# Side work of a fused attention and FP4 block set at other places in its slots, and two of three zeroings of K tiles put later in the start

## What is computed

```
xn   = layernorm(x)                                  # no gain, no bias, eps 1e-5
q    = rope(xn @ Wqa @ Wqb)   16 heads of 8          # low-rank projections
k, v = xn @ Wkva @ Wkvb       4 heads of 8; k = rope(k)
attn = softmax(causal(q k' / sqrt(8))) v @ Wout + bout
fp4(t): blocks of 16 along the last dim, scale = max|t| / 6,
        round |t| / scale to 0, .5, 1, 1.5, 2, 3, 4, 6, times sign and scale
ffn  = fp4(silu(fp4(xn) fp4(Wgate)') * (fp4(xn) fp4(Wup)')) fp4(Wdown)'     # 352 hidden
out  = x + attn + ffn
```

## Time and profile before

| | us |
|---|---|
| median of 3 runs (788.24 to 791.44) | 790.27 |
| the profiled execution, whole | 788.24 |
| its span, first to last instruction | 785.8 |

### The profile page before, as it was taken

How to read it: one execution, slowest core, us unless ns; L and a number is a source line. 1 busy time by engine, 2 the same in 40 slices (tenths; PEclk the granted TensorE clock), 3 DMA queues, 4 the chain that set the end, 5 groups by cost and what they waited for, 6 DMA issues and landing times.

```text
span 785.8 us, 18291 instructions
## 1 busy us (share of the span) xinstructions
PE 718.4 (91%) x6453; PEld 440.8 (56%) x6453; DVE 627.7 (80%) x1424; ACT 535.9 (68%) x1154; POOL 588.6 (75%) x630
## 2 busy tenths in 40 slices
PE   2467899999999999999999999999999999999886
PEld 1233455665656565665656565665656565665443
DVE  6569888889798888989798888989798888878412
ACT  2213676867777777867777777877777777777772
POOL 4533597878879797868889797878788797856662
PEclk9999899999999999999999999999999999999999
DMA  4432224334334433344334334243334333241111
GB/s 111 108 77 82 67 76 109 93 106 113 99 93 117 103 114 97 94 106 113 97 94 119 104 109 105 89 117 104 96 99 126 94 117 95 77 115 46 57 50 49
DMA packets 84885, 75.41 MB, mean 96 GB/s; under 512 B 28627, under 2 KB 66868, under 8 KB 84796
## 3 DMA queue, kind: packets, MB, share of 16 engines
q1 hardware_dynamic: 84796, 74.25, 35.1%
HBM read 40.38 MB, written 27.25 MB: 86 GB/s over the span
## 4 chain that ended last, share of the span: by engine, by line
PE 62%; DVE 15%; ACT 7%; POOL 6%; issue 4%; DMA 3%; SPq 2%; POOLq 0%; DVEq 0%; ACTq 0%
PE pv_ps L1159 16%; PE exp_ps L1137 12%; PE max_ps L1122 8%; DVE neg_max L732 7%; PE misc_ps L1183 5%; PE max_ps L1123 5%; PE misc_ps L1220 5%; ACT P L958 3%; PE misc_ps L1191 3%; PE misc_ps L1208 3%; PE misc_ps L1218 2%; POOL P L555 2%; PE misc_ps L1169 1%; DVE h_mag L694 1%; PE misc_ps L1187 1%
## 5 line engine op out<-in xcount | busy, mean ns | idle before, releaser
L732 DVE TENSOR_REDUCE neg_max<-max_ps 128x1 f32<-128x512 f32 (+3 forms) x768 | 430.4, 593 | 88.2 <-PE max_ps L1123 86.1
L958 ACT ACTIVATE P<-exp_ps 128x512 f32<-128x512 f32 x512 | 294.7, 599 | 164.0 <-PE exp_ps L1137 163.0
L1137 PE MATMUL exp_ps<-Q,K 128*128 128x512 bf16 (+3 forms) x1024 | 243.4, 301 | 10.2 <-ACT P L958 6.8
L1122 PE MATMUL max_ps<-K,Q 128*128 128x384 bf16 (+2 forms) x768 | 198.9, 278 | 20.1 <-DMA Kd<-K 10.5
L1123 PE MATMUL max_ps<-Kd,Q 128*128 128x128 bf16 x1024 | 190.7, 220 | 1.4 <-DVE neg_max L732 1.2
L555 POOL TENSOR_SCALAR_AFFINE_SELECT P<-P 128x512 f32<-128x512 f32 x256 | 161.7, 667 | 30.6 <-ACT P L961 30.6
L1159 PE MATMUL pv_ps<-P,V 128*32 128x512 f32 (+3 forms) x2048 | 163.9, 438 | 1.2 <-POOL P L555 0.8
L1122 PEld LDWEIGHTS max_ps<-K,Q 128*128 128x128 bf16 x768 | 75.6, 99 | 97.6 <-DVE neg_max L732 53.8
L1123 PEld LDWEIGHTS max_ps<-Kd,Q 128*128 128x128 bf16 x1024 | 99.0, 100 | 42.5 <-issue 22.7
L1137 PEld LDWEIGHTS exp_ps<-Q,K 128*128 128x128 bf16 x1024 | 79.6, 98 | 48.0 <-ACT P L958 26.4
L586 POOL TENSOR_TENSOR h<-gate_sb,up_half 128x352 f32<-128x352 f32 x64 | 59.5, 930 | 54.6 <-DVE gate_sb L745 54.5
(11 more groups left out here) (126 smaller groups left out, 962.7 us busy)
## 6 DMA issues: line engine op xcount, KB each, us to landing
Q<-q_scr SPq DMA_DIRECT2D x64, 224.0 KB
o_scr<-oT SPq DMA_DIRECT2D x31, 256.0 KB, 3.3
q_scr<-q_split SPq DMA_DIRECT2D x16, 384.0 KB, 2.6
Kd<-K SPq DMA_DIRECT2D x64, 96.0 KB
x_in<-x SPq DMA_DIRECT2D x16, 256.0 KB, 4.7
q_scr<-q_split SPq DMA_DIRECT2D x16, 256.0 KB, 2.9
x_res<-x SPq DMA_DIRECT2D x16, 256.0 KB, 5.7
out<-y SPq DMA_DIRECT2D x32, 128.0 KB, 4.4
```

The costliest lines, as they stand in the source:

```text
L732: nc.vector.tensor_reduce(neg_max[:, pr // 4, heads[0]:heads[0] + len(heads), pr % 4, i], max_ps[r % 3][:, 0:len(heads) * n].rearrange("p ...
L958: nc.scalar.activation(P[g % 2][:, hh + r % 2, col:col + 512], ps[:, :], ACT.Exp, scale=SCALE).then_inc(exp_done, 1)
L1122: nc.tensor.matmul(ps[:, col:col + d], Qt, Kt[:, half, g, 0:d], start=True, stop=True)
L1137: last = nc.tensor.matmul(exp_ps[n % 2][:, col:col + width], K[par][:, half, pr // 2, kb * 128:(kb + 1) * 128], Q[par][:, pr, kb * 128:S], ...
```

## The change

Seven edits, none of which changes what is computed:

- DVE, start: of the three zeroings only K[1]'s stays ahead of the iterations. K[0] is cleared in iteration -3 behind var_eps, Kd in the same iteration behind the scales of x.
- DVE, statistics: two of the four bn_stats move to the end of slot 1, with the wait for x; bn_aggr and var_eps move ahead of one more reduction each; a new `neg_mean` (-1 times the mean) is made beside var_eps.
- POOL: `shift` = neg_mean times rstd is computed there, behind the power, instead of on DVE in front of slot 5.
- DVE, slot 0: the x magnitudes go behind the sixth reduction instead of the fifth. ACT: the cast x_mag goes from behind exp tile 0 to behind exp tile 2.
- DVE, slot 4: one reduction is put between the two halves of the h magnitudes.
- ACT: the four h_mag casts each move one place later.
- PE, slot 3: the first three v chunks each move one tile later.

```diff
-H_POWERS = [(2, 2), (2, 3), (2, 4), (3, 2)]
+H_POWERS = [(2, 3), (2, 4), (3, 2), (3, 4)]
...
-                T.wait(pool, var_done, 1, 3, 1)
+                T.wait(pool, var_done, 2, 3, 2)
                 nc.gpsimd.tensor_tensor(rstd[:, :], var_eps[:, :], half_neg[:, :], ALU.pow).then_inc(rstd_done, 1)
+                T.wait(pool, rstd_done, 2, 3, 1)
+                nc.gpsimd.tensor_tensor(shift[:, :], neg_mean[:, :], rstd[:, :], ALU.mult).then_inc(rstd_done, 1)
...
+            def clear_keys(k):
+
+                nc.vector.memset(k[:, :, :, :].bitcast(F32), 0.0).then_inc(k_zeroed, 1)
...
                 reduces(0, 4)
+                reduces(0, 5)
                 if T.has(2):
                     T.wait(dve, x_powers, 1, 2, 1)
                     magnitudes(lambda s, n: T.wait(dve, s, 2, 2, n), x_mag[:, :], x_mags)
-                reduces(0, 5)
...
                 reduces(1, 5)
+                if T.has(3):
+                    T.wait(dve, x_loaded, 16, 3, 16)
+                    for c in range(2):
+                        nc.vector.bn_stats(bn_raw[:, c, :], x_in[:, c, :]).then_inc(bn_done, 1)
...
                 if T.has(3):
-                    T.wait(dve, x_loaded, 16, 3, 16)
-                    for c in range(NT):
+                    for c in range(2, NT):
                         nc.vector.bn_stats(bn_raw[:, c, :], x_in[:, c, :]).then_inc(bn_done, 1)
                 reduces(3, 2)
                 gated(T, 2)
-                reduces(3, 3)
                 if T.has(3):
                     for c in range(NT):
                         T.wait(dve, bn_done, NT, 3, c + 1)
                         dve.sem_inc(dve_marks, 1)
                         nc.vector.bn_aggr(bn_mv[:, c, :], bn_raw[:, c, :]).then_inc(mv_done, 1)
-                reduces(3, 4)
+                reduces(3, 3)
                 if T.has(3):
                     T.wait(dve, mv_done, NT, 3, NT)
 
                     T.wait(dve, rstd_done, 2, 2, 1)
+                    T.wait(dve, rstd_done, 2, 2, 2)
+                    nc.vector.tensor_scalar(neg_mean[:, :], bn_mv[:, :, 0], -1.0, None, ALU.mult).then_inc(var_done, 1)
                     nc.vector.tensor_scalar(var_eps[:, :], bn_mv[:, :, 1], EPS, None, ALU.add).then_inc(var_done, 1)
+                if T.t0 == FIRST_T:
+
+                    clear_keys(K[0])
+                reduces(3, 4)
                 reduces(3, 5)
...
-                    magnitudes(lambda s, n: T.wait(dve, s, 2, 0, n), h_mag[:, :], h_mags)
-                reduces(4, 1, 2)
+                    magnitude_bits(h_mag[:, :], h_mags)
+                reduces(4, 1)
+                if T.has(0):
+                    magnitude_floor(lambda s, n: T.wait(dve, s, 2, 0, n), h_mag[:, :], h_mags)
+                reduces(4, 2)
...
-                if T.has(3):
-                    T.wait(dve, rstd_done, 2, 3, 1)
-                    nc.vector.scalar_tensor_tensor(shift[:, :], bn_mv[:, :, 0], -1.0, rstd[:, :],
-                                                   ALU.mult, ALU.mult).then_inc(rstd_done, 1)
...
                     scales(lambda s, n: T.wait(dve, s, 4, 3, n), x_max[:, :], x_scale[:, :], x_inv[:, :], x_scales)
+                if T.t0 == FIRST_T:
+                    clear_keys(Kd)
...
-            for k in (K[0], K[1], Kd):
-                nc.vector.memset(k[:, :, :, :].bitcast(F32), 0.0).then_inc(k_zeroed, 1)
+            clear_keys(K[1])
...
-                if (slot, r) == (0, 0) and T.has(2):
+                if (slot, r) == (0, 2) and T.has(2):
                     T.wait(act, x_scaled, 1, 2, 1)
...
                     values = slot == 3 and T.has(2)
+                    max_tile(T, slot, 4)
                     if values:
                         value_chunk(T, 0)
-                    max_tile(T, slot, 4)
+                    exp_tile(T, slot, 4)
                     if values:
                         value_chunk(T, 1)
-                    exp_tile(T, slot, 4)
+                    max_tile(T, slot, 5)
                     if values:
                         value_chunk(T, 2)
-                    max_tile(T, slot, 5)
```

More of the change, by code:

```diff
@@ L173, in build @@
         rstd = sb("rstd", [128, NT])
+        neg_mean = sb("neg_mean", [128, NT])
         shift = sb("shift", [128, NT])
@@ L685, in scales, with magnitude_bits, magnitude_floor, magnitudes @@
                 nc.vector.tensor_scalar(inv, inv, 1.0 - 2.0 ** -22, None, ALU.mult).then_inc(sem_, 1)
-            def magnitudes(eng_wait, mag, sem_):
+            def magnitude_bits(mag, sem_):
                 m = mag.bitcast(U16)
                 nc.vector.tensor_scalar(m, m, 0x7F80, 0x0040, ALU.bitwise_and, ALU.bitwise_or).then_inc(sem_, 1)
+            def magnitude_floor(eng_wait, mag, sem_):
                 eng_wait(sem_, 1)
                 nc.vector.tensor_scalar(mag, mag, 1.5 * 2.0 ** 22, None, ALU.max).then_inc(sem_, 1)
+            def magnitudes(eng_wait, mag, sem_):
+                magnitude_bits(mag, sem_)
+                magnitude_floor(eng_wait, mag, sem_)
             def weight_scales():
```

## The result

| | before | after |
|---|---|---|
| median, us (5 runs each) | 789.1 (788.24 to 791.44) | 794.5 (793.42 to 795.95) |
| ratio of after to before, with its 95% interval | | 1.0063 (1.0048 to 1.0078) |
| the profiled execution, whole | 788.24 | 793.81 |
| its span | 785.8 | 791.6 |

The changed kernel is 0.63% slower. The stretches of its trace, in the same order as in the earlier trace rows (start, iteration -1, fourteen batches, t0 = 3, t0 = 5), are these; columns are length, then busy us of PE, weight loads, DVE, ACT and POOL, then clock, DMA share and GB/s. Some of PE's records are missing from this trace (396 of 403 in a batch), so its busy time isn't compared.

The account below looks back on a forecast made before the run. The start was taken as one chain, slots 3 to 7 as bound by GpSimd's chain. Terms 8.3 - 0.35 + 0.3 + 0 - 0.3 - 0.1 = +7.9 us gave 796.1 profiled, 798 median; range 791 to 804.

Parts of the forecast that it names:

- the last batches: The last batches of the kernel: a gain of 0.1 us in the sum.
- the middle outcome: Time within about 4 us of no change, 786.3 to 794.2: Rival (i) and Rival (iv), chance 0.18.
- (a): Start: moving two zeroings ends the scales at 13.5, not 14.47, but SyncE's constants issue 1.95 us later.
- (b): Start, t0 = -2: early statistics wait for batch 1's x, moving q_sin from 22.21 to 30.5, +8.3 us.
- Rival (iv): Start: batch 1's x arrives in time, so the statistics' stall doesn't come; 789.5 us, chance 0.03.
- (c): Batch t0 = -1: x_mag bits behind the sixth reduction, after GpSimd's product is over; 0.35 us gained.
- (d): Slot 0 of every batch: later x_mag cast lets up_half come earlier; 0.29 us gained a batch.
- (e): Slots 3 to 7: GpSimd's longer chain costs 0.3 us a batch; TensorE's savings become waiting ahead of hqT0.
- Rival (iii): Slot 3: var_eps falls into q_split in most batches, 0.67 us more each; 806 us, chance 0.12.
- (f): Other batches: t0 = 0 +0.3 us; t0 = 1 to 12 0; t0 = 5's stall perhaps not recurring, -0.3.
- Rival (i): Steady batches gain after all, -6 us in 12 batches, about outweighing the start; 792 us, chance 0.16.

Follow-up runs that it names:

- Experiment 2: The changed kernel with all three zeroings ahead of the iterations again, the early statistics kept in slot 1; 791.87 us, ratio 1.0042.
- experiment 1: The changed kernel with all four bn_stats back in slot 3 in iteration t0 = -2 alone; 785.82 us, ratio 0.9965.
- Experiment 4: The kernel before with only the x magnitudes moved (cast behind exp tile 2, bits behind the sixth reduction); 787.19 us, ratio 0.9977.
- experiment 7: The kernel before with only the negated mean added on VectorE and the shift product moved to GpSimd; 793.02 us, ratio 1.0036.
- experiments 9: Changed kernel with t0 = -2 statistics back in slot 3, GpSimd's last masks split around h's product, slot 3's value chunks one tile earlier; 778.78 us, ratio 0.9858.
- 10: Changed kernel with t0 = -2 statistics back in slot 3, GpSimd's last masks split, h magnitudes' floor behind slot 4's third reduction; 777.28 us, ratio 0.9839.
- Experiments 3: The changed kernel with the shift product issued twice on GpSimd, the second behind the first; 798.8 us, ratio 1.0126.
- Experiment 8: The changed kernel with t0 = -2 statistics back in slot 3 and the four h_mag casts at their old places; 786.89 us, ratio 0.9959.

## Why the prediction was right, and where it was off

Slower was right, by the mechanism forecast, and the time is in the range. The sum had +7.9 us for the profiled execution (796.1); it took 793.81, +5.6. My 798 had 2 us more on top, for a median that lay above the profiled run by 2.0; with five runs of each kernel that distance was 0.9 before and 0.7 after. So of the 3.5 us that I was over, 2.3 are the sum's and 1.2 come from the step to the median, for which three executions were a thin base. The sum came nearer than its terms did: the start, t0 = -1, t0 = 0, t0 = 5 and the other eleven batches were each taken too high, by 2.8 us in all, and the last batches too low by 0.7. That these errors work against each other is luck. (The chance of the middle outcome is given as 0.18; its parts, 0.16 and 0.03, make 0.19.)

**(a) Zeroings.** Right. The copy at 7.04 (6.95 forecast), the scales' end at 13.55 (13.5), SyncE's constants at 15.71 (15.7). The point I left open, whether the K[0] clear would hold GpSimd, is decided: the power began at 9.03, the zeroing at 9.31, and the power took 1.02 us. Experiment 2 prices the slip at 2.2 us of the stall, where the slip alone (13.73 to 15.71) is 2.0.

**(b) The statistics' wait.** Right in place, kind and nearly in size: q_sin at 30.04 for 30.5, +7.8 us for +8.3. The step that was too long: I took 11.78 us from the first constant's issue to x's, as in the earlier trace rows, and it was 11.08 (11.16 in experiment 2). The issuing takes 8.4 us in all three; the landing of the constants, for which SyncE waits, ended 3.4 us behind it before and 2.7 us in both others. The wait for x's landing gave 0.24 us of this back (2.84 for 2.6). The idle stretch of "some 10 us" was 10.35, the first reduction moved by 7.73, the first max tile to 51.99 (52.5 forecast), and experiment 1 took 8.45 us off with this one edit. Rival (iv) is gone: x is still issued behind the constants.

**(c) t0 = -1.** -0.56 for -0.35. The bits of x_mag took 0.31 us in the new place, as forecast (0.29 beside an idle GpSimd, against 0.64 in the earlier trace rows). But the bits don't explain the stretch. Experiment 4 has them short (0.29) and t0 = -1 longer than before (37.93); experiment 7 has them at 0.64 as before and t0 = -1 at 36.78, 0.57 shorter. So what shortened it is open, and that the term came out near is no proof of it.

**(d) Slot 0.** Right: -0.33 for -0.29. The transposes of xn now follow their exp pair in 0.21 us, where the earlier trace rows had 0.51:

```profile
222.63 0.38 PE L1158 MATMUL exp_ps<-Q,K 128*128 128x384 bf16 x2
222.84 0.61 PE L1208 MATMUL misc_ps<-ident,xn 128*128 128x128 f32 x4
```

Experiment 4 shows it alone (-0.33 in slot 0, -0.34 in the period).

**(e) Slots 3 to 7.** The sum was right (+0.24 for +0.3: 27.68 to 27.92), and so was its reason: GpSimd from q_split's start to h's end takes 18.72 us, and 18.48 in the earlier trace rows (234.62 to 253.10). Its parts fell differently. From the batch t0 = 3, to be laid beside the earlier trace rows:

```profile
239.62 0.39 PE L1158 MATMUL exp_ps<-Q,K 128*128 128x256 bf16 x2 [0.28 <-ACT P L979]
239.77 0.93 POOL L587 TENSOR_TENSOR h<-gate_sb,up_half 128x352 f32<-128x352 f32 x1 [0.18 <-DVE gate_sb L758]
240.34 0.39 DVE L895 TENSOR_SCALAR neg_mean<-bn_mv 128x4 f32<-128x4 f32 x1
240.64 0.16 DVE L896 TENSOR_SCALAR var_eps<-bn_mv 128x4 f32<-128x4 f32 x1
241.03 1.16 POOL L647 TENSOR_TENSOR q_split<-q_rest,q_split 128x512 bf16<-128x512 f32 x1 [0.33 <-ACT q_split L1074]
242.15 2.68 POOL L556 TENSOR_SCALAR_AFFINE_SELECT P<-P 128x512 f32<-128x512 f32 x4
242.88 0.87 DVE L693 TENSOR_SCALAR h_mag<-h_mag 128x1408 uint16<-128x1408 uint16 x1
244.27 0.94 DVE L698 TENSOR_SCALAR h_mag<-h_mag 128x1408 bf16<-128x1408 bf16 x1
245.72 0.29 PE L1144 MATMUL max_ps<-Kd,Q 128*128 128x128 bf16 x2 [0.20 <-DVE neg_max L745]
246.55 0.20 POOL L608 TENSOR_TENSOR shift<-neg_mean,rstd 128x4 f32<-128x4 f32 x1
257.16 2.59 POOL L572 TENSOR_TENSOR h<-h,h_scale 128x1408 f32<-128x1408 f32 x1
259.89 0.52 PE L1229 MATMUL misc_ps<-ident,h 128*128 128x128 f32 x3
```

Slot 3 is 0.23 us worse by its wait for ScalarE, as forecast (0.2), and the shift takes 0.20 on GpSimd (0.24). Slot 4 is where a step failed: "there the wait moves on to the exp tile". It moved to the last max tile. Both halves of the h magnitudes now lie beside GpSimd's masks and take 0.87 and 0.94 us, 1.81 together, where they took 0.52 and 0.84 before; the reduction behind them came late, as the row at 245.72 shows. That the bits are held too comes from the moved value chunks (experiments 9 and 10). So TensorE saved less in slot 4 than I thought (5.58 for 5.83; experiment 7, with the old value chunks and magnitudes, has 5.23), reached hqT0 later, and the wait there was about 0.2 us from start to start and no 0.4 to 0.6. That left the period alone, as GpSimd sets it. Experiments 3 and 7 carry the reading: more on GpSimd comes out in full, and 0.6 us saved by TensorE in slot 4 comes back as a wait.

**Rival (iii)** did not come: the negated mean at 240.34 waited for GpSimd's product (0.39 us, to its end at 240.70), and var_eps, at 240.64, was done 0.2 us ahead of q_split. In this batch the sums' DMA was 0.46 us late; in most others var_eps ends 0.46 us ahead, and 0.10 us in the worst of the softmax batches (t0 = 9). The list of its instances (duration ns minimum/median/maximum) shows that it was never held, while before the one in the earlier trace rows took 0.99 us:

```profile
L896 DVE TENSOR_SCALAR var_eps<-bn_mv x16: 154/156/164, 8.8 to 634.9; 128x4 f32<-128x4 f32 x16
```

**(f) The other batches.** The mis-sized terms. t0 = 0: -0.19 for +0.3. I had taken GpSimd's +0.3 there without slot 0's -0.3, but that is not shown to be the reason: experiment 4, with slot 0's gain alone, has +0.33 there, and experiment 7, with GpSimd's cost alone, -0.20. The other eleven batches gave -1.1 in all, for 0: slot 0's gain is 0.33 and GpSimd's cost 0.24, and their difference of 0.1, which I had rounded away, counts ten times (t0 = 12 gave 0.01). t0 = 5: -0.73 for -0.3; its event did not come again. Rival (i) thus had the right sign and a third of the size.

**The last batches** were +0.62 for -0.1, with the wrong sign like t0 = 0: t0 = 13 gave -0.15, and the end +0.77. 0.3 us of it lie ahead of GpSimd's product on the sums of the softmax, which waits for a DMA and starts that much later in relation to the iteration. The rest lies at the last masks. The changed kernel:

```profile
776.98 2.86 POOL L556 TENSOR_SCALAR_AFFINE_SELECT P<-P 128x512 f32<-128x512 f32 x4 [3.44 <-ACT P L982]
778.66 0.68 DVE L796 TENSOR_TENSOR onT<-o_raw,o_spread 64x512 f32<-64x512 f32 x1 [6.11 <-DMA o_spread<-i_scr]
```

The kernel before:

```profile
771.72 2.39 POOL L555 TENSOR_SCALAR_AFFINE_SELECT P<-P 128x512 f32<-128x512 f32 x4 [3.44 <-ACT P L961]
773.72 0.93 DVE L783 TENSOR_TENSOR onT<-o_raw,o_spread 64x512 f32<-64x512 f32 x1 [6.00 <-DMA o_spread<-i_scr]
```

Both have four masks and one product of VectorE at the end of them. Before, the product took 0.93 us and the masks 2.39; after, the product 0.68 and the masks 2.86, and the last weighted sums wait for the masks. It looks as if the one that starts first makes the other wait: before, the product started 0.24 us behind the last mask, after, 0.08 us ahead of it. Experiment 8 had the masks as after (2.84, the product 0.74), experiment 1 as before (2.40; its product, at 0.68, starts 0.5 us behind the last mask), and they differ in casts that have nothing to do with it. The start of the product hangs on a DMA's landing, and the end varies from 87.7 to 89.4 us over the kernels here. So this is argued and not shown; it isn't a cost which I can put down to an edit.

## What to carry to other kernels

A wait belongs where its data are late in the worst iteration, not in the usual one: the statistics waited for x once in the changed kernel's sixteen batches, in the filling iteration, where the load stands behind one-time work of another queue, and that once cost 8.5 us. Moving one-time work behind the critical engine's own needs pays only if nothing critical waits for what a second queue brings behind that work: the moved zeroings delayed x by 1.3 us, which cost nothing in experiment 1, and 2.2 us of the start where VectorE waited for x. In a batch in which TensorE is 98% busy, look for the slower chain that ends right on one of its waits, and lighten that first: once the wait for it (0.19 us a batch) was gone, two other placements gave 0.60 more. And an operation that another engine can hold up should have some room behind it: var_eps with 0.11 us to spare was caught in a batch whose DMA came 0.4 us late, with 0.46 us it was not.

## What the runs showed of the hardware

VectorE's zeroing of 128x2048 float32 took 1.76 us beside GpSimd's power and did not hold it (1.02 us, begun 0.28 us before it); operations on four columns next to a GpSimd product did wait (0.39, 0.92 and 0.99 us for work of 0.16). That the floor, a bfloat16 operation with one input, should be among those that GpSimd's masks hold up (0.94 us for 0.52) I had not expected, and taking it from beside them was worth 0.38 us a batch. The bits, an operation on 16-bit integers, were held in the same way (0.87 us for 0.52). The Trainium skill (SBUF — State Buffer, section Who interferes with whom) has VectorE instructions in a two-port mode among those that exclude GpSimd's for their whole length, and these durations agree; no run here tells the modes apart. TensorE's idle time is a poor price for a wait: 0.13 us idle in slot 0 was worth 0.33 when it went, 0.20 us in slot 4 some 0.4 (5.57 to 5.16 with the floor moved), and 0.28 us in slot 3 only 0.22 (5.91 to 5.69 with the value chunks back).
